# Twelve of each chunk's 64 C-row products in the Mamba mixers: from VectorE to GpSimd, with their scans written to SBUF

## The reference

```
def step(h, inp):
    dt_t, B_t, C_t, x_t = inp
    dA = jnp.exp(dt_t[..., None] * A)
    h = dA * h + (dt_t * x_t)[..., None] * B_t[:, None, :]
    y = jnp.einsum('ben,bn->be', h, C_t)
    return (h, y)
...
y = ssm_scan(dt, Bm, Cm, xc, A) + xc * Dp
y = y * jax.nn.silu(z)
return jnp.einsum('ble,de->bld', y, outproj)
```

## Time and profile before

| | |
|---|---|
| median of 3 runs | 3511.59 us (3508.27 to 3514.30) |
| profiled execution | 3526.84 us, its span 3524.6 us |
| mean granted clock of TensorE | 0.905 |
| busy over the span | PE 2867.8, DVE 2089.9, ACT 1436.8, POOL 1370.2 us |
| `scan` L490, 768 times | 468.5 + 490.5 us |
| `weigh` L506, 768 times | 519.5 us |
| `term` L750, 768 times | 975.0 us |
| `decay` L639, 768 times | 526.5 us |

### The profile page before, as it was taken

How to read it: one execution, slowest core, us unless ns; L and a number is a source line. 1 busy time by engine, 2 the same in 40 slices (tenths; PEclk the granted TensorE clock), 3 DMA queues, 4 the chain that set the end, 5 groups by cost and what they waited for, 6 DMA issues and landing times. The chain is left out here.

```text
span 3524.6 us, 30222 instructions
## 1 busy us (share of the span) xinstructions
PE 2867.8 (81%) x8560; PEld 1248.7 (35%) x8560; DVE 2089.9 (59%) x2977; ACT 1436.8 (41%) x2168; POOL 1370.2 (39%) x1138
## 2 busy tenths in 40 slices
PE   5888988888775877999999829999478887779966
PEld 1232332333222543222222228888132332226522
DVE  1899999999995436444444230000339999932233
ACT  4566556655643322333333302221246555422233
POOL 2588788778774012000000140000437788720010
PEclk8999999999998978999999959999589999986688
DMA  1222022012200002100100224444221022000000
GB/s 62 94 96 93 26 96 102 32 71 96 79 18 18 1 14 90 28 19 20 26 18 19 69 97 142 179 180 142 79 96 63 35 96 96 0 18 0 0 7 24
DMA packets 67914, 215.28 MB, mean 61 GB/s; under 512 B 15517, under 2 KB 40361, under 8 KB 48697
## 3 DMA queue, kind: packets, MB, share of 16 engines
q1 hardware_dynamic: 61384, 181.12, 14.4%
q10 hardware_dynamic: 3312, 24.12, 2.0%
q0 software_dynamic: 3072, 8.39, 0.7%
HBM read 187.97 MB, written 25.43 MB: 61 GB/s over the span
## 5 line engine op out<-in xcount | busy, mean ns | idle before, releaser
L750 POOL TENSOR_TENSOR s_dbu<-s_dx,s_bc 128x512 f32<-128x512 f32 x768 | 975.0, 1275 | 313.3 <-DVE s_psum L490 312.3
L420 PE MATMUL s_psum<-s_hc,ident 128*128 128x512 f32 x1536 | 850.2, 638 | 209.9 <-DVE s_hc L506 209.1
L639 ACT ACTIVATE s_psum<-s_dt,s_a_neg 128x512 f32<-128x512 f32 x768 | 526.5, 690 | 631.0 <-DVE s_hc L506 630.2
L506 DVE TENSOR_TENSOR s_hc<-s_psum,s_bc 128x512 f32<-128x512 f32 x768 | 519.5, 677 | 0.9 <-issue 0.6
L420 PEld LDWEIGHTS s_psum<-s_hc,ident 128*128 128x128 f32 x1536 | 240.0, 190 | 764.4 <-DVE s_hc L506 686.0
L490 DVE TENSOR_TENSOR_SCAN s_psum<-s_psum,s_state,s_dbu 128x512 f32<-128x512 f32 x384 | 490.5, 1277 | 10.2 <-ACT s_psum L639 10.2
L490 DVE TENSOR_TENSOR_SCAN s_psum<-s_psum,s_dbu 128x512 f32<-128x512 f32 x384 | 468.5, 1220 | 12.8 <-ACT s_psum L639 9.9
L1329 DVE TENSOR_REDUCE s_umax<-s_banks 128x1 f32<-128x512 f32 (+3 forms) x384 | 210.3, 554 | 282.6 <-PE s_banks L1195 223.5
L1233 PE MATMUL s_banks<-s_probs,s_vs 128*17 128x512 f32 (+3 forms) x768 | 324.4, 512 | 35.6 <-ACT s_ot L1410 32.3
L1419 ACT ACTIVATE s_probs<-s_banks 128x512 f32<-128x512 f32 (+3 forms) x384 | 187.3, 489 | 395.7 <-PE s_banks L1219 295.5
L1780 ACT ACTIVATE s_hidden<-s_banks,s_w 128x256 f32<-128x256 f32 x184 | 77.1, 470 | 302.8 <-PE s_banks L1603 302.8
(11 more groups left out here) (249 smaller groups left out, 3626.0 us busy)
## 6 DMA issues: line engine op xcount, KB each, us to landing
s_bc<-fwd_rows SPq DMA_DIRECT2D x64, 1024.0 KB, 4.8
s_bc<-m_rows SPq DMA_DIRECT2D x32, 1024.0 KB, 4.7
s_w<-in_moe_w SPq DMA_DIRECT2D x23, 1028.0 KB, 7.3
s_w<-in_moe_w ACTq DMA_DIRECT2D x23, 1024.0 KB, 5.6
s_stack<-qk_parts SPq DMA_DIRECT2D x192, 64.0 KB, 2.1
qk_parts<-s_parts SPq DMA_DIRECT2D x48, 128.0 KB, 1.8
moe_in_rows<-s_zero SPq DMA_DIRECT2D x1, 5888.0 KB, 19.1
s_xs<-moe_in_rows SPq DMA_DIRECT2D x23, 256.0 KB, 6.0
```

The lines of the kernel that those rows point to most:

```text
L420: pe.matmul(psum[:, SCANS + block_no % 2, :], consts["ident"][:], hc[:, unit % PRODUCTS, :], start=(n == 0), stop=(n == NS - 1)).then_inc( ...
L506: dve.tensor_tensor(hc[:, unit % PRODUCTS, :], psum[:, unit % SCANS, :], bc[:, 2 * n + 1, :], ALU.mult)\
L639: act.activation(psum[:, unit % SCANS, :], dt[:, g % 2, i // NS, :], ACT.Exp, scale=a_neg[CHUNKS[g][0]][:, i:i + 1]).then_inc(decay_ready, 1)
L750: pool.tensor_tensor(dbu[:, unit % TERMS, :], dx[:, g % 2, i // NS, :], bc[:, 2 * n, :], ALU.mult)\
```

## The change

A list `LENT` marks 12 of a chunk's 64 units: i = 2, 6, 10, ..., 46. For these units:

- VectorE's scan writes into a new SBUF tile `hs` [128 x 512] instead of back into its PSUM bank, and waits for the lent product before it (one buffer).
- VectorE skips `weigh`. In keep chunks its `keep` behind it copies only the odd unit's column.
- GpSimd does `weigh_lent`: in keep chunks a copy of the last column of `hs` to `state`, then `hs` times the C row into the same ring `hc`. It stands in GpSimd's queue ahead of the term three units later.
- ScalarE's decay of four units later waits for the scan alone.
- TensorE's `total` waits on a semaphore of its own, `product_lent`. Waits that count products count the two kinds apart (`own`, `lent`).

```diff
+LENT = [i < 3 * NS and i % 4 == 2 for i in range(UNITS)]
+
+def lent(units):
+    return units // UNITS * sum(LENT) + sum(LENT[:units % UNITS])
+
+def own(units):
+    return units - lent(units)
...
+        hs = s.sb("hs", [P, CH])
...
-                        sp.wait_ge(product_ready, (g + 1) * UNITS - NS + n + 2)
+                        sp.wait_ge(product_ready, own((g + 1) * UNITS - NS + n + 2))
...
-                pe.wait_ge(product_ready, unit + 1)
+                if LENT[i]:
+                    pe.wait_ge(product_lent, lent(unit + 1))
+                else:
+                    pe.wait_ge(product_ready, own(unit + 1))
...
                 if CHUNKS[g][2] and i == 0:
                     dve.wait_ge(kept, (g + 1) // 2 * (UNITS // 2))
+                    dve.wait_ge(kept_lent, (g + 1) // 2 * sum(LENT))
...
-                dve.tensor_tensor_scan(h, h, dbu[:, unit % TERMS, :], begin, ALU.mult, ALU.add).then_inc(scanned, 1)
+                if LENT[i] and lent(unit):
+                    dve.wait_ge(product_lent, lent(unit))
+                dve.tensor_tensor_scan(hs[:] if LENT[i] else h, h, dbu[:, unit % TERMS, :], begin, ALU.mult, ALU.add)\
+                   .then_inc(scanned, 1)
...
-                dve.tensor_copy(state[:, i - 1:i + 1].unsqueeze(2), psum[:, at - 1:at + 1, CH - 1:CH]).then_inc(kept, 1)
+                if LENT[i - 1]:
+                    dve.tensor_copy(state[:, i:i + 1], psum[:, at, CH - 1:CH]).then_inc(kept, 1)
+                else:
+                    dve.tensor_copy(state[:, i - 1:i + 1].unsqueeze(2), psum[:, at - 1:at + 1, CH - 1:CH]).then_inc(kept, 1)
...
-                    if unit:
+                    if unit and not LENT[(unit - 1) % UNITS]:
                         weigh(unit - 1)
...
-                if unit >= SCANS:
-                    act.wait_ge(product_ready, unit - SCANS + 1)
+                if unit >= SCANS and LENT[(unit - SCANS) % UNITS]:
+                    act.wait_ge(scanned, unit - SCANS + 1)
+                elif unit >= SCANS:
+                    act.wait_ge(product_ready, own(unit - SCANS + 1))
...
+            def weigh_lent(unit):
+
+                i = unit % UNITS
+                pool.wait_ge(scanned, unit + 1)
+                if unit >= PRODUCTS:
+                    pool.wait_ge(product_used, unit - PRODUCTS + 1)
+                if CHUNKS[unit // UNITS][2] + 1 < BCH:
+                    pool.tensor_copy(state[:, i:i + 1], hs[:, CH - 1:CH]).then_inc(kept_lent, 1)
+                pool.tensor_tensor(hc[:, unit % PRODUCTS, :], hs[:], bc[:, 2 * (i % NS) + 1, :], ALU.mult)\
+                    .then_inc(product_lent, 1)
...
+                    if i >= TERMS and LENT[i - TERMS]:
+                        weigh_lent(g * UNITS + i - TERMS)
                     term(g, i)
```

More of the change, by code:

```diff
@@ L279, in mixers @@
                                                         s.sem("y_read"), s.sem("y_ready"))
+        product_lent, kept_lent = s.sem("product_lent"), s.sem("kept_lent")
         squared, rstd_ready, normed, x_added = (s.sem("squared"), s.sem("rstd_ready"), s.sem("normed"),
```

## The result

| | before | after |
|---|---|---|
| median | 3510.43 us (4 runs, 3508.27 to 3514.30) | 3454.89 us (4 runs, 3448.55 to 3457.00) |
| ratio | | 0.9838 (95% interval 0.9821 to 0.9855) |
| span of the profiled execution | 3524.6 us | 3453.9 us |
| both Mamba pipelines | 1465.3 us | 1407.4 us |

The change makes the kernel 55.5 us faster; 59.3 was forecast. "Both pipelines" is the time from the start of the first scan to the end of the last in stage 0, and the same in stage 3, added up from the scans' starts in the timeline (before: 985.0 + 480.3, after: 947.9 + 459.5). They are 57.9 us shorter. What lies outside them isn't touched by any kernel here, and it took between 2037 and 2059 us in their profiled executions, so the two spans differ by more (70.7 us) than the change brings.

A forecast was written before the change was run, and what follows sets the result against it. VectorE's queue was taken to bound the mixer chunks. 85.0 saved less 14.8 (gates), 6.3 (ScalarE's chain), 1.9 (chunk ends) and 2.7 (`scale_in`) gave 59.3 us: 3511.6 - 59.3 = 3452.3, forecast 3452, range 3433 to 3483.

The forecast's parts named there:

- VectorE's queue is the pace: Mixer chunks last as long as VectorE's queue; removing 12 weighings of 0.59 us a chunk saves 85 us over 12 chunks.
- Part 2: Lent scans writing to SBUF instead of PSUM: taken as 0, bounds -4 to +9 us for 144 scans.
- Rival B: More is lost: dearer SBUF scans (9), no overlap of neighbouring scans (6), TensorE bound (12), giving 3480 us; chance 0.24.
- Part 3: GpSimd gains 12 multiplications a chunk, 1.27 us each; 6.13 a group against VectorE's 6.53, so it fits in plain stretches.
- (a): GpSimd's four `times_gate` at units 3 to 9 make it late: 1.6 us per state chunk, 1.3 per keep chunk, 14.8 together.
- (b): ScalarE's chain from decay 41 to 45 doesn't shorten, so part of the saving between scans 38 and 45 is lost: 6.3 us.
- (c): From unit 47 on GpSimd runs without a gap: 1.3 us lost in chunk 9, 0.2 in chunks 0, 8, 10; 1.9 together.
- `scale_in`: Four such GpSimd operations, 1.53 us each to the next start, in chunks 2 and 4: cost 0.4 and 2.3 us.
- TensorE at 0: TensorE needs 6.9 us per four units against VectorE's 6.53 in units 0 to 27; costed at 0, 12 us if it binds.
- A: Nearly all is kept, leads absorbing the gates and ScalarE's chain: 85 less about 7, giving 3434 us; chance 0.12.
- C: The scan's SBUF write blocks GpSimd for 1.2 us; slower by 30 us, 3542; decides from 1.0 us extra per lent unit; chance 0.08.
- D: The gain goes elsewhere: GpSimd's lateness holds products and buffers so all engines wait in turn, 3512 us within 7; chance 0.06.

The follow-up runs named there:

- gates_only: The changed kernel with only units 2, 6 and 10 lent (3 of 64): 3507.2 us, 0.9981 of the kernel before.
- half: The changed kernel with every second lent unit kept (2, 10, 18, ... 42; six of 64): 3484.8 us, 0.9925 of the kernel before.
- no_gate_units: The changed kernel without lent units 2 and 6 (ten of 64 left): 3450.3 us, 0.9805 of the kernel before.
- no_42: The changed kernel without lent unit 42 (eleven left): 3457.4 us, 0.9836 of the kernel before.
- to_the_end: The changed kernel with units 50, 54 and 58 lent too (15 of 64): 3473.3 us, 0.9883 of the kernel before.
- double_lent: The changed kernel with GpSimd computing each lent product twice into the same buffer: 3576.2 us, 1.0186 of the kernel before.
- sbuf_only: The changed kernel with the lent units' scans still writing to SBUF, but VectorE weighing them itself: 3588.8 us, 1.0209 of the kernel before.
- spread: The changed kernel with exp_var moved behind decay 46 and scale_in of chunks 2 and 4 moved later: 3448.5 us, 0.9817 of the kernel before.

## Why the prediction was right, step by step

- **VectorE's queue is the pace**: right. A group of four units without a stall (28 to 31) takes 6.51 us in chunk 5 and 6.70 in chunk 6, where 6.53 and 6.75 were forecast. In gates_only, half, no_gate_units, no_42, to_the_end and double_lent the time moved by what VectorE's queue lost or another queue imposed, within 7 us of what was expected, but for double_lent's 15.
- **Part 2, SBUF target at 0**: right. 1.214 and 1.275 against 1.220 and 1.277, and neighbouring scans start 1.19 apart. Rival B's terms for these came to 0.
- **Part 3, a lent product at 1.27, GpSimd fitting in the plain stretches**: right. The timeline of chunk 5 from unit 16 on shows no wait for GpSimd; no weighing of chunk 5 waited for `product_used`.
- **(a) The gates**, 1.6 (state) and 1.3 (keep): the first 16 units of chunk 1 went from 29.11 to 28.42, of chunk 6 from 30.16 to 29.00, so of 2.36 us 1.67 and 1.20 were lost. The 14.8 us of the sum were about right, and no_gate_units and gates_only show the place. (For a state chunk the sum's own terms add up to 18.8 and not 18.7, which makes no difference here.) VectorE's new waits for GpSimd are 14.3 less the 2.8 of before plus the 3.4 marked `issue`, 14.9 us, where "about 15" was written; some 4 of them stand not at the gates but beside `scale_in` and at the ends of chunks.
- **(b) ScalarE's stretch**: the chain and the size right, the share of each product wrong. Scans 38 to 45 became 0.56 us shorter in state chunks (0.4 forecast) and 0.61 in keep chunks (0.75 forecast), a loss of 6.6 us in all where the sum has 6.3. ScalarE's rows in chunk 5 of the changed kernel, decay 41, then decays 43 and 44, then 45 and 46:

```profile
768.60 0.69 ACT L664 ACTIVATE s_psum<-s_dt,s_a_neg 128x512 f32<-128x512 f32 x1
...
772.78 1.29 ACT L664 ACTIVATE s_psum<-s_dt,s_a_neg 128x512 f32<-128x512 f32 x2
...
779.81 1.28 ACT L664 ACTIVATE s_psum<-s_dt,s_a_neg 128x512 f32<-128x512 f32 x2
```

The 0.45 us of idle time ahead of decay 44 in the earlier trace rows is gone. ScalarE now runs from decay 41 to 45 without a gap, 11.2 us, and scan 45 starts 13.82 us after scan 38, as the chain of the sum has it (13.9). What the step left out is that decay 44 also waits for weighing 40, the idle time that the earlier trace rows shows. The product of unit 38 stands ahead of weighing 40 and closes that gap, and in keep chunks, where weighing 40 still ends last (by 0.09 us in chunk 2), its 0.6 is all there is to gain. The product of unit 42 stands behind weighing 40: half and no_42 show that it is worth 0. The sum cut both products together and so could not tell the useful one from the useless one; that the keep chunks' 0.75 came out near is luck, in so far as no term of the sum knows of weighing 40.
- **(c) The end of a chunk**: chunk 9's last eight units grew by 1.02 us (1.3 forecast), the one state chunk with little lead; the others by 0 to 0.4, and chunk 6's 0.4 is one weighing that started 0.29 us late. to_the_end shows that the margin was thin. `scale_in` in chunk 4: its first 16 units rose from 30.16 to 31.34, a loss of 3.5 us with the gates' 1.3, as forecast (3.6); chunk 2 lost about 1 instead of 0.4.
- **`scale_y`**: missing. The prediction read its 1.040 us (742 to 1404 ns) as a sign that VectorE and GpSimd hinder each other, but put no term for it in the sum. In chunks 1 to 6 the second `scale_y` went from 1.39 (state) and 1.17 us (keep) to 1.79, so the product of unit 46 brings 0.2 us or nothing there; in chunk 7 it went from 1.39 to 0.72. That is 2.4 us lost in all. It didn't show in the total because each product gave VectorE 0.61 us in a plain group, not 0.59 (2.9 us over 144): that the sum missed by only 1.4 us is in part luck.
- **TensorE at 0**: right here. In each kernel between none and three of the weighings started late, by 0.2 to 0.3 us; in the changed kernel it was one of 624.
- **The rivals.** A and B gave 3434 and 3480; the interval excludes both. C, an SBUF write that blocks GpSimd, is refuted by GpSimd's durations: 1.269 and 1.272 us in the median of all, and none of the 173 that overlapped a lent scan took more than 1.31. Its price was sound: double_lent put 1.35 us on each product and ended slower than before. D's 3512 within 7 is outside the measured range too.

The Trainium skill (SBUF — State Buffer, Who interferes with whom) says that a VectorE instruction with two SBUF inputs contends with a GpSimd instruction that reads SBUF, that the shared ports are an exclusive lock and the order of issue decides who is blocked, and that a VectorE instruction with one SBUF input, outside the two-port modes, doesn't contend. sbuf_only agrees: 1.72 us for the weighing that started 0.09 us late, 1.63 for the term that did, and a median of 0.674 (0.660 to 0.709) for the 624 weighings with one input in PSUM.

The Trainium skill's advice (GPSIMD Engine Reference, Engine selection) against elementwise work on GpSimd is right on the price (1.27 to 0.68 us) and would have misjudged this change: the dearer instruction stands where its engine was idle.

What stays open: the first eight units of chunks 0 and 8 differ from kernel to kernel by more than their lists of lent units explain (chunk 8: 12.94 us in spread, 13.85 in the changed kernel, with the same list). What makes single weighings start 0.2 to 0.3 us late isn't shown either.

## What to carry to other kernels

Count for each engine what its queue costs, start to start, over the stretch between two points where the engines must meet; a move from the longest queue to another pays stretch by stretch, and nothing where the receiver's queue is already as long or where a third engine's chain begins ahead of the saving. Fewer moves, placed where there is room, gave more than a regular pattern: ten products a chunk beat 12, and 15 lost nearly half of the gain. Hand the receiver data in SBUF only if the giver need not read it again beside it. And look at the instructions of the giver that already read two SBUF tiles: a busier receiver changes when they meet its own.

## What the runs showed of the hardware

- Two SBUF inputs on VectorE beside a GpSimd multiplication (sbuf_only): 0.67 us becomes 1.72 in the median and up to 1.79 when GpSimd's is already running; when VectorE's starts first, it keeps its 0.68 and GpSimd's 1.27 becomes 1.63. A shift of 0.3 us decides who pays: in state chunks the weighing starts 0.18 us before the term; in keep chunks, where two column copies stand between scan and weighing, 0.09 after it. State chunks lost 1.8 to 2.3 us, keep chunks 10.7 to 11.8.
- In the changed kernel the same thing hits `scale_y`: 1.79 us where it starts 0.03 us behind a term, 0.72 in chunk 7.
- A scan of 128x512 costs the same into SBUF as into PSUM (1.214 and 1.221 us in the changed kernel), and GpSimd's multiplications keep their 1.27 us beside it.
